# Attention: score and maximum products over all 128 partition rows instead of 98 and 96, with the spare rows cleared

## What is computed

```python
q, k, v = jnp.moveaxis(qkv, 2, 0)
attn = jnp.einsum('blhd,bmhd->bhlm', q, k) * HD ** (-0.5)
attn = jax.nn.softmax(attn, axis=-1)
out = jnp.einsum('bhlm,bmhd->blhd', attn, v).reshape(B, L, D)
```

## Time and profile before

| | |
|---|---|
| median of 3 runs | 3310.24 us (3308.21 to 3312.79) |
| profiled execution, its time | 3309.95 us |
| its span | 3308.2 us |
| mean granted TensorE clock | 0.981 of full speed |
| busy: PE, DVE, ACT, POOL | 3173.0, 1947.7, 1568.8, 1620.3 us |
| attention | from 800.8 us to about 2440 us of the span |

### The profile page before, as it was taken

How to read it: one execution, slowest core, us unless ns; L and a number is a source line. 1 busy time by engine, 2 the same in 40 slices (tenths; PEclk the granted TensorE clock), 3 DMA queues, 4 the chain that set the end, 5 groups by cost and what they waited for, 6 DMA issues and landing times. The chain is left out here.

```text
span 3308.2 us, 44377 instructions
## 1 busy us (share of the span) xinstructions
PE 3173.0 (96%) x16788; PEld 2165.2 (65%) x16788; DVE 1947.7 (59%) x3352; ACT 1568.8 (47%) x2879; POOL 1620.3 (49%) x800
## 2 busy tenths in 40 slices
PE   7899989998999999999999999999979799999998
PEld 5788877776555555555555555555438688888887
DVE  2477764465878778787787787787436322222221
ACT  0122224432666666666666666666645432222221
POOL 2366530000778778788788787787863000000000
PEclk9999989998999999999999999999989899999999
DMA  5143324635568767778667687667467421111100
GB/s 196 56 133 99 120 71 169 199 148 163 146 158 189 172 152 166 171 162 196 161 150 175 165 179 177 152 159 178 116 180 267 165 74 42 42 42 41 41 20 13
DMA packets 198866, 446.93 MB, mean 135 GB/s; under 512 B 65871, under 2 KB 87631, under 8 KB 167942
## 3 DMA queue, kind: packets, MB, share of 16 engines
q1 hardware_dynamic: 140006, 250.23, 22.3%
q0 software_dynamic: 18432, 134.23, 20.5%
q10 hardware_dynamic: 40224, 59.78, 7.7%
HBM read 157.39 MB, written 84.44 MB: 73 GB/s over the span
## 5 line engine op out<-in xcount | busy, mean ns | idle before, releaser
L1345 DVE TENSOR_REDUCE heads_mx<-att_pM 128x1 f32<-128x512 f32 x1984 | 1214.3, 679 | 325.2 <-PE att_pM L1400 324.2
L1330 ACT ACTIVATE att_prob<-att_pS 128x512 f32<-128x512 f32 x2048 | 1047.5, 618 | 360.9 <-PE att_pS L1447 354.4
L1263 POOL TENSOR_TENSOR att_acc<-att_acc,att_prob 128x2048 f32<-128x2048 f32 x224 | 1034.8, 4620 | 204.1 <-ACT att_prob L1330 193.6
L1415 PE MATMUL att_pO<-att_prob,att_V 128*32 128x512 f32 x4096 | 492.7, 598 | 0.0
L1447 PE MATMUL att_pS<-heads_q,heads_k 98*128 98x512 f32 x1024 | 424.2, 414 | 7.1 <-DMA heads_q<-att_nm 7.1
L1447 PE MATMUL att_pS<-att_qs,att_ks 98*128 98x512 f32 x1024 | 423.9, 418 | 2.4 <-ACT att_prob L1330 2.1
L1400 PE MATMUL att_pM<-att_ks,att_qs 96*128 96x512 f32 x1024 | 408.4, 399 | 0.0
L1400 PE MATMUL att_pM<-heads_k,heads_q 96*128 96x512 f32 x960 | 388.3, 409 | 3.4 <-PEq L107 3.4
L1985 PE MATMUL mlp_pu<-mlp_hs,mlp_W 128*128 128x512 f32 x1536 | 371.8, 391 | 12.4 <-POOL mlp_hs L1928 12.4
L1985 PEld LDWEIGHTS mlp_pu<-mlp_hs,mlp_W 128*128 128x128 f32 x1536 | 290.3, 189 | 73.4 <-POOL mlp_hs L1928 12.8
L1915 ACT ACTIVATE mlp_tu<-mlp_pu,keep_cols 128x512 f32<-128x512 f32 x128 | 88.3, 690 | 505.3 <-PE mlp_pu L1985 505.3
(11 more groups left out here) (237 smaller groups left out, 3723.3 us busy)
## 6 DMA issues: line engine op xcount, KB each, us to landing
att_gathered<-att_prob POOLq DMA_DIRECT2D x128, 1024.0 KB, 8.2
att_gathered<-att_prob SPq DMA_DIRECT2D x64, 1024.0 KB, 6.2
qk_d<-graph_LW SPq DMA_DIRECT2D x64, 512.0 KB, 2.8
heads_q<-qk_d ACTq DMA_DIRECT2D x21, 512.0 KB
heads_k<-qk_d ACTq DMA_DIRECT2D x21, 512.0 KB
att_qs<-qk_d ACTq DMA_DIRECT2D x21, 512.0 KB, 7.1
att_ks<-qk_d ACTq DMA_DIRECT2D x21, 512.0 KB, 10.5
gat_xT<-in_xT SPq DMA_DIRECT2D x32, 256.0 KB, 3.3
```

The source lines that it names most:

```text
L1263: nc.gpsimd.tensor_tensor(acc[half][:], old[:], new[:], ALU.add).then_inc(added, 1)
L1330: nc.scalar.activation(prob[step % PR][:, c, :], pS[at % 3][:], ACT.Exp, scale=SCALE).then_inc(exp_done, 1)
L1345: nc.vector.tensor_reduce(mx[:, q // 4, q % 4:q % 4 + 1], bank(at)[:], AX.X, ALU.max).then_inc(m_read, 1)
L1415: last = nc.tensor.matmul(pO[c * HD:(c + 1) * HD, :], V[g % 2][:, mt, (c // 2) * HD:(c // 2 + 1) * HD], prob[step % PR][:, c, :], start=mt ...
```

## The change

Both products take all 128 rows. So that the spare rows add nothing, POOL now clears rows 96 to 127 of both q and both k buffers before it writes the ones into rows 96 and 97 of k: per buffer three memsets instead of one. PE waits for all of them before its first maximum product instead of before its first score product. Since the maximum product now sees rows 96 and 97, those of q must be zero again whenever a new group's q has been loaded: a seventh DMA per load (`i == 6`) copies the cleared rows 98 and 99 of the same q buffer over rows 96 and 97. ACT issues it in step 3, behind the two loads there; at the start SP issues it for group 1, after it has waited for the memsets, and SP waits for them again before `rows(0)`. PE's wait for the loads goes from 96 to 112 per use of a buffer.

```diff
-        LOADS = [1, 1, 2, 2, 3, 3]
+        LOADS = [1, 1, 2, 2, 3, 3, 3]
...
-        qs = [keep["a_q"][0:KD + 2], m.sb("qs1", [KD + 2, 2, S], F32R)]
-
-        ks = [keep["a_k"][0:KD + 2], m.sb("ks1", [KD + 2, 2, S], F32R)]
+        qs = [keep["a_q"], m.sb("qs1", [P, 2, S], F32R)]
+
+        ks = [keep["a_k"], m.sb("ks1", [P, 2, S], F32R)]
...
         def load_part(eng, g, i):
             k, at = g % U, slice(g % 2 * S, (g % 2 + 1) * S)
-            if i < 3:
+            if i == 6:
+                dst, src = qs[k][KD:KD + 2], raw(qs[k][KD + 2:KD + 4])
+            elif i < 3:
...
             def load(g):
-                for i in range(6):
+                for i in range(7):
+                    if i == 6:
+                        sp.wait_ge(cleared, 1 + 3 * U)
                     load_part(sp, g, i)
...
             load_v(1)
+            sp.wait_ge(cleared, 1 + 3 * U)
             rows(0)
...
             for k in range(U):
-                pool.wait_ge(cleared, 1 + k)
+                pool.wait_ge(cleared, 1 + 3 * k)
+                nc.gpsimd.memset(raw(qs[k][KD:P]), 0.0).then_inc(cleared, 1)
+                pool.wait_ge(cleared, 2 + 3 * k)
+                nc.gpsimd.memset(raw(ks[k][KD:P]), 0.0).then_inc(cleared, 1)
+                pool.wait_ge(cleared, 3 + 3 * k)
                 nc.gpsimd.memset(raw(ks[k][KD:KD + 2]), 1.0).then_inc(cleared, 1)
...
-                for i in range(6):
+                for i in range(7):
                     if step == LOADS[i]:
                         load_part(act, g + 1, i)
...
-                    pe.wait_ge(loaded[k], (g + k) // U * 96)
+                    pe.wait_ge(loaded[k], (g + k) // U * 112)
                 wait_bank(pe, at)
                 h, t, mc = q // 32, q // 4 % 8, q % 4
-                nc.tensor.matmul(bank(at)[:], qs[k][0:KD, h, (half * 8 + t) * P:(half * 8 + t + 1) * P], ks[k][0:KD, h, mc * 512:(mc + 1) * 512],
+                nc.tensor.matmul(bank(at)[:], qs[k][:, h, (half * 8 + t) * P:(half * 8 + t + 1) * P], ks[k][:, h, mc * 512:(mc + 1) * 512],
                                  start=True, stop=True).then_inc(m_done, 1)
...
+            pe.wait_ge(cleared, 1 + 3 * U)
             for q in range(EARLY):
                 maxima(1, q)
             top_of(0)
             for q in range(EARLY, LEAD * 4):
                 maxima(1, q)
-            pe.wait_ge(cleared, 1 + U)
```

More of the change, by code:

```diff
@@ L1202, in _ @@
                 else:
-                    sp.wait_ge(cleared, 3 + U)
+                    sp.wait_ge(cleared, 3 + 3 * U)
                     sp.wait_ge(o_stored, 64 * (2 * NG - 2))
@@ L1220, in _ @@
             for k in range(U):
-                pool.wait_ge(cleared, 1 + k)
+                pool.wait_ge(cleared, 1 + 3 * k)
[3 more added lines that the diff above has]
+                pool.wait_ge(cleared, 3 + 3 * k)
                 nc.gpsimd.memset(raw(ks[k][KD:KD + 2]), 1.0).then_inc(cleared, 1)
             for i, tile in enumerate((keep["p_heads_r"], keep["p_zt"])):
-                pool.wait_ge(cleared, 1 + U + i)
+                pool.wait_ge(cleared, 1 + 3 * U + i)
                 nc.gpsimd.memset(raw(tile), 0.0).then_inc(cleared, 1)
-            pool.wait_ge(cleared, 3 + U)
+            pool.wait_ge(cleared, 3 + 3 * U)
             def send(n, i, j):
@@ L1319, in _ @@
                     act.wait_ge(weights_early, 16 * (DC + B + 2))
-                    act.wait_ge(cleared, 2 + U)
+                    act.wait_ge(cleared, 2 + 3 * U)
                     nc.scalar.activation(keep["p_heads_r"][0:2 * H, :], keep["p_heads"][0:2 * H, :], ACT.Identity)
```

## The result

The changed kernel takes 3325.61 us (median of 6 runs, 3323.45 to 3326.94) against 3310.16 for the kernel before (6 runs, 3307.4 to 3313.09): ratio 1.0047, 95% interval 1.0034 to 1.0059, that is 15.5 us slower. The span of its profiled execution is 3324.9 us, 16.7 more than before's 3308.2. In what follows the lines of attention stand some 9 higher: L1447 is now L1456, L1400 is L1409, L1415 is L1424. Some comparisons hold single spells in which TensorE's clock was granted at half; where one matters it is named.

The account below looks back on a forecast made before the run. PE seemed the bound, but at ACT's pace by the end of every window. -2.5 + 14.2 + 6.3 = +18.0 us on 3309.95 gave 3328.0, written as 3328 us; range 3322 to 3334, chance 0.70.

Parts of the forecast that it names:

- The start, +14.2: Start of attention: PE's early maximum products wait for six memsets, moving the first score from 822.21 to 836.4; +14.2 us.
- The copy, +6.3: Step 3 of 14 groups: ACT's seventh load issue counts in full, 0.45 us each; +6.3 us, bounds 4.3 and 17.2.
- The rows, -2.5: 248 windows with maximum products: equal rows shorten only two pitches, 0.010 us together; -2.5 us, bounds 0 and -3.5.
- The 50 ns of the Trainium skill: Copy's issue on ACT: the skill's sequencer cost per DMA would make the term 0.7 us; the prediction argued against it.
- the eighth score's load would still wait for the fifth exponential: End of each window: even with faster products, this weight load waits for ACT until 1506.89 at the latest.
- The larger claim: Attention windows: by the end of each, PE runs at ACT's pace, so it cannot use the 0.227 us pitch.
- The pitch gain is real everywhere: All 4032 attention products gain 0.007 us, ACT following; windows shorten by more than 0.11 us, total 3302.2; chance 0.06.
- Half of it: Attention windows get shorter by 0.04 to 0.08 us, total 3311 to 3321; chance 0.10.
- A drain at each change of rows: Attention products: possible mechanism of the first rival, were 96 and 98 rows two tiling modes; 0.234 us pitch hardly fits.
- The clear is dear: ACT's copy of cleared rows in 14 groups issues in 1.23 us like `rows(n)`, total 3339; chance 0.12.
- The change does nothing to PE: Attention pitch stays at 0.234 us, slowed by the stall behind each pack; total 3330.7, no separate chance.

Follow-up runs that it names:

- The first experiment: Only the six memsets and PE's wait for them ahead of its first maximum product, against the kernel before; products stay at 98 and 96 rows: 3323.95 us, ratio 1.0048.
- short exponentials: Each exponential takes 256 of 512 columns, in the kernel before (3305.01 us) and in the changed kernel without the copy of the rows (3303.15 us).

## Why the prediction was right, and where it was not

The forecast was 3328 us, 17.8 slower; measured is 15.5 slower. Direction and size are right; the terms are less good than their sum, which owes its closeness in part to luck: the copy cost 4.7 us more than forecast, the rows gave 1.8 more, and the clock gave back most of the rest.

*The start, +14.2.* Right in every step: memsets of 3.51 us whatever the rows, the last one over at 821.9 (822.3 forecast), the early products 14.1 us, the first score at 836.06 (836.4 forecast), no wait for `rows(0)`, whose issues took 2.72 us instead of the 4.9 assumed. The first experiment shows the delay alone. The clock was taken to stand at half for 5.6 us of the scores; it did for 1.4, which gave about 1.4 us back in group 0, a little more than the +-1 allowed for.

*The copy, +6.3.* The mechanism was right: ACT has no slack behind two loads, and the third issue is exposed in full. The size was not: the issue takes 0.60 us (median), alone in its step or behind two loads, not the 0.45 of the k loads that it was said to resemble. That 0.45 is moreover not the price of a k load but of any load issued right behind another; a load by itself takes 0.31. A group pays 0.78, so the term is 14 x 0.78 = 11.0 us, inside the bounds of 4.3 and 17.2 and above the 9 of the forecast's own range. The 50 ns of the Trainium skill ("DMA: Bandwidth & Descriptors", section "Anatomy of one DMA — SWDGE (gpsimd) path") stand there for DMAs that GpSimd issues, and the prediction should not have carried them over to ACT; ACT's queue shows 598 ns at least for the copy.

*The rows, -2.5.* The size came out near, at 100.75 - 100.46 = 0.29 us in a group, 4.3 us over 15 groups, a little beyond the bound of -3.5. The reasoning behind it failed in one step: "the eighth score's load would still wait for the fifth exponential", and therefore nothing inside the chain could be gained. The load does wait (3.212 in every full kernel), but the product behind it does not depend on the load alone. With unequal rows it came 0.173 us behind its load, held by the pitch behind the maximum product before it; with equal rows it comes 0.155 behind. The larger claim, that ACT is what keeps PE from 0.227 us, held for part of the windows only. In the same-buffer windows it is so: with equal rows the last four pitches are 0.233 us with full exponentials and 0.227 with short ones. In those behind step 10 the pitch is 0.233 without ACT in the way too. The conclusion (no large gain) is right, but only in part for the reason given.

*The rivals.* "The pitch gain is real everywhere" did not come: windows shrank by 0.025 us, not 0.11, and "Half of it" (0.04 to 0.08) did not either. The premise, that unlike rows are what slows PE, is true for those 0.025. A drain at each change of rows, as a reading of the Trainium skill's "TensorEngine Tiling (Array Packing)", Key Properties, would have it, does not show in 0.001 us per product. "The clear is dear" came part of the way: the issue takes 0.60 us against its 1.23, and a group pays 0.78. "The change does nothing to PE" was nearly right on the pitch (0.2341 to 0.2326), but 14 such pitches in a window make up most of this term's 4.3 us. Its reason, the stall behind each pack, does not by itself hold PE back for a whole window: in the same-buffer windows with equal rows and short exponentials PE recovers.

The terms as measured give 14.25 + 11.0 - 4.3 = 21 us. The two traces differ by 16.7, and the rest is nearly all the clock's or outside attention: 1.4 in group 0, 2.1 behind group 15 with a spell of half clock fewer, 0.2 in group 15 and 0.4 us in front. The medians are 15.5 apart; the 1.2 us between that and the traces need no cause, since the six runs of a kernel lie 5.7 us (before) and 3.5 us (changed) apart.

## What to carry to other kernels

When a phase begins with memsets behind a barrier, look up who needs which piece first: the same clearing cost 14.3 us as one wait and 0.8 us cut and ordered. A DMA issue on an engine that is near its limit costs its issue time where it stands behind others and, here, a quarter of that where it stood alone and the engine waited anyway; count issues per step before adding one, and check that the landing still beats its first use. A pitch that differs between two phases by a few nanoseconds is not yet a gain to be had: take the suspected limits away, one and then both, and look at each kind of window by itself: here the median over all windows said that nothing moved, while one kind reached the better pitch.

## What was not expected of the hardware

- Two streams of products in turn with unequal row counts (98 and 96, or 128 and 96) make the windows some 0.02 us longer than with equal ones (98 and 98, or 128 and 128); 128 is no better than 98.
- With equal rows and ACT out of the way, the pitch in the same-buffer windows settles at 0.227 us from the twelfth product behind a pack on; with 98 and 96 rows in turn it stays at 0.233.
- A wait long fulfilled and a raised semaphore on every product leave the pitch at 0.227 us.
- Behind transposes of another shape, products over 128 rows need up to ten products until their pitch settles at 0.227.
- ACT needs 0.60 us to issue a copy of two rows inside SBUF, wherever it stands; a load of 512 KB takes 0.31 us by itself and 0.45 right behind another (medians).
